# B turned to tokens by a block transposition and SBUF copies instead of four matrix transpositions

## The reference, cut to what matters

```
Y_diag = einsum('bcln,bcsn,bhcls,bcshp->bclhp', C, B, L, x*dt)
states = einsum('bcln,bhcl,bclhp->bchpn',       B, decay, x*dt)
Y_off  = einsum('bcln,bchpn,bhcl->bclhp',       C, states_prev, exp(Acs))
```

## Time and profile before

| | |
|---|---|
| median of 3 runs | 3097.44 us (3097.33 to 3103.48) |
| the profiled execution | 3100.98 us, its span 3099.3 us |
| mean granted TensorE clock | 0.988 of 2.4 GHz |
| TensorE busy | 3020.9 us (97%), 21504 matmuls |
| VectorE busy | 2378.1 us (77%) |
| GpSimd busy | 2047.3 us (66%) |
| ScalarE busy | 1912.2 us (62%) |
| DMA engines, SP's queue | 136608 packets, 210.05 MB, 20.8% of 16 engines |

### The profile page before, as it was taken

How to read it: one execution, slowest core, us unless ns; L and a number is a source line. 1 busy time by engine, 2 the same in 40 slices (tenths; PEclk the granted TensorE clock), 3 DMA queues, 4 the chain that set the end, 5 groups by cost and what they waited for, 6 DMA issues and landing times.

```text
span 3099.3 us, 65999 instructions
## 1 busy us (share of the span) xinstructions
PE 3020.9 (97%) x21504; PEld 2600.8 (84%) x21504; DVE 2378.1 (77%) x5136; ACT 1912.2 (62%) x4117; POOL 2047.3 (66%) x2311
## 2 busy tenths in 40 slices
PE   5799999999999999999999999999999999999997
PEld 4688888888888888888888888888888888888876
DVE  5877887777887778787778777778777778777762
ACT  5566665666666666666566666556666566656562
POOL 2477666677666677666677666677666776666774
PEclk7999999999999999999999999999999999999998
DMA  3123222223222223222222222222222222222221
GB/s 126 42 70 90 75 82 62 68 68 89 75 75 68 68 68 89 75 66 69 70 74 82 79 68 62 65 88 78 79 68 61 68 89 77 80 62 68 68 83 42
DMA packets 153547, 227.36 MB, mean 73 GB/s; under 512 B 30624, under 2 KB 98976, under 8 KB 153504
## 3 DMA queue, kind: packets, MB, share of 16 engines
q1 hardware_dynamic: 136608, 210.05, 20.8%
q0 software_dynamic: 16896, 16.78, 3.8%
HBM read 174.87 MB, written 35.13 MB: 68 GB/s over the span
## 4 chain that ended last, share of the span: by engine, by line
PE 86%; POOL 7%; DVE 1%; issue 1%; DMA 1%; ACT 0%; SPq 0%; POOLq 0%; DVEq 0%; ACTq 0%
PE fpb L1443 32%; PE apb L1443 19%; PE acc L1623 16%; PE apb L1576 4%; PE apb L1452 4%; PE apb L1559 2%; PE ppb L1443 2%; PE apb L1566 2%; POOL hid L653 1%; PE ppb L1462 1%; POOL hidL L658 1%; PE fpb L1492 1%; PE fpb L1494 1%; PE apb L1546 1%; POOL xD L628 1%
## 5 line engine op out<-in xcount | busy, mean ns | idle before, releaser
L658 POOL TENSOR_TENSOR hidL<-hid,hidH 128x512 fp32r<-128x512 f32 x384 | 559.2, 1456 | 204.1 <-ACT hidH L913 196.2
L913 ACT CAST hidH<-hid 128x512 fp32r<-128x512 f32 x384 | 236.6, 616 | 422.0 <-POOL hid L653 312.7
L1129 DVE SCALAR_TENSOR_TENSOR xc<-apb,cw,xc 128x511 f32<-128x511 f32 (+2 forms) x576 | 428.0, 747 | 73.3 <-ACT xc L833 45.4
L1623 PE MATMUL acc<-WDH,hidH 128*128 128x256 f32 x1536 | 457.5, 298 | 5.9 <-POOLq L660 4.8
L1623 PE MATMUL acc<-WDL,hidH 128*128 128x256 f32 x1536 | 430.2, 280 | 0.0
L1623 PE MATMUL acc<-WDH,hidL 128*128 128x256 f32 x1536 | 430.2, 280 | 0.0
L653 POOL TENSOR_TENSOR hid<-hid,cb 128x512 f32<-128x512 f32 x256 | 347.5, 1357 | 40.2 <-DMA cb<-c_row 15.8
L1248 DVE TENSOR_TENSOR hid<-hid,fpb 128x512 f32<-128x512 f32 x384 | 260.2, 678 | 127.4 <-PE fpb L1443 114.6
L1443 PE MATMUL fpb<-fTh,UH 128*128 128x512 f32 x768 | 336.8, 439 | 0.0
L1443 PE MATMUL fpb<-fTh,GH 128*128 128x512 f32 x768 | 317.5, 413 | 0.0
L851 ACT ACTIVATE seg<-seg,acs 128x128 f32<-128x128 f32 x1024 | 313.4, 389 | 4.1 <-POOL seg L613 3.8
(11 more groups left out here) (191 smaller groups left out, 8544.6 us busy)
## 6 DMA issues: line engine op xcount, KB each, us to landing
seg<-acs_row SPq DMA_DIRECT2D x128, 512.0 KB, 4.3
cb<-c_row SPq DMA_DIRECT2D x512, 128.0 KB, 2.9
xsP<-in_x SPq DMA_DIRECT2D x32, 512.0 KB, 3.7
xc<-qrot SPq DMA_DIRECT2D x32, 512.0 KB, 3.4
xc<-in_x SPq DMA_DIRECT2D x32, 512.0 KB, 4.4
out<-xc SPq DMA_DIRECT2D x32, 512.0 KB, 2.9
out<-xn POOLq DMA_DIRECT2D x32, 512.0 KB, 6.1
ZL_loaded<-in_wzx_t SPq DMA_DIRECT2D x2, 512.0 KB, 4.6
```

Of the source, the lines that this page charges most:

```text
L658: own.do(G.tensor_tensor(hidL[:, j % 2, :], hid[:, j % 2, :], hidH[:, j % 2, :].bitcast(fp32), ALU.subtract))
L913: A.copy(hidH[:, j % 2, :], hid[:, j % 2, :]).then_inc(sem["hidden_high"], 1)
L1129: ins = V.scalar_tensor_tensor(xc[:, b, s:], src[:, 0:T - s], cw[:, b, TAPS - 1 - s:TAPS - s], xc[:, b, s:], ALU.mult, ALU.add)
L1623: ins = nc.tensor.matmul(dst, l[:, w, tk], r[:, j, :], start=j == 0 and t % 2 == 0 and n == 0, stop=j == HB - 1 and n == 2, skip_group_che ...
```

## The change

VectorE transposes `xc[:, 4, :]` in 32x32 blocks into `ysp` (`turn_B`), once ScalarE has finished `conv_silu(4)`. Each block is then turned, but lies in the wrong quadrant: 32 channels of quadrant q on the partitions of q. SP issues sixteen DMAs inside SBUF (`spread_B`), one for each pair of quadrants, 32 partitions by 4 chunks by 32 values (16 KB) each, which put the blocks into `Btok`. `state(0)` waits for all sixteen. `B_by_token`, `evac_B` and the slot "Bt" are gone. `turn_B` stands behind `conv(0)` in the loop, behind `conv(1)` in the fill and behind `up(0)` in the tail; `spread_B` stands ahead of `decay_store` everywhere.

```diff
             "qn_ready": ("PE", "p", 2, False), "hh_ready": ("DVE", "p", 2, False),
 
+            "B_made": ("DVE", "a", 1, False), "B_turned": ("SP", "a", 1, False),
+            "B_spread": ("PE", "a", 16 * (P // Q) ** 2, False),
...
+            def spread_B():
+
+                sp.wait_ge(sem["B_turned"], 1)
+                turned = ysp[:].rearrange("p (t u r) -> p t u r", u=P // Q, r=Q)
+                for q in range(P // Q):
+                    for u in range(P // Q):
+                        sp.dma_start(Btok[u * Q:(u + 1) * Q, :, q * Q:(q + 1) * Q], turned[q * Q:(q + 1) * Q, :, u, :]
+                                     ).then_inc(sem["B_spread"], 16)
...
             def first(i):
-                decay_store(); decay_rows(0); load_next(i + 1); decay_rows(1); decay_rows(2); decay_rows(3)
+                spread_B(); decay_store(); decay_rows(0); load_next(i + 1); decay_rows(1); decay_rows(2); decay_rows(3)
...
             def iteration(i, g=True):
-                save_x1(i - 1); decay_store(); decay_rows(0); decay_rows(1); combine_store(); combine_rows(0)
+                save_x1(i - 1); spread_B(); decay_store(); decay_rows(0); decay_rows(1); combine_store(); combine_rows(0)
...
             def conv_silu(b):
                 act.wait_ge(sem["conv_ready"], way.plan.conv.index(b) + 1)
-                free("a", f"xc{b}", A.activation(xc[:, b, :], xc[:, b, :], ACT.Silu))
+                ins = A.activation(xc[:, b, :], xc[:, b, :], ACT.Silu)
+                if b == 4:
+                    own.do(ins)
+                    act.sem_inc(sem["B_made"], 1)
+                    freed["a"].append("xc4")
+                    act.sem_inc(sem["a_out_ACT"], 1)
+                else:
+                    free("a", f"xc{b}", ins)
...
-            def evac_B():
-                way.filled(act, "ACT", "Bt")
-                free("a", "Bt", A.copy(Btok[:].rearrange("p t n -> p (t n)"), way.bank("Bt")[:]))
...
+            def turn_B():
+                dve.wait_ge(sem["B_made"], 1)
+                V.transpose(ysp[:].rearrange("p (b r) -> p b r", r=Q), xc[:, 4, :].rearrange("p (b r) -> p b r", r=Q)
+                            ).then_inc(sem["B_turned"], 1)
...
-            def B_by_token():
-                b = slot("Bt")
-                read_out("xc4")
-                fill("Bt", transposes(b, lambda t: xc[:, 4, t * P:(t + 1) * P]))
...
             def state(c):
                 b = slot(f"st{c}")
                 if c == 0:
-                    read_out("Bt")
+                    pe.wait_ge(sem["B_spread"], 16 * (P // Q) ** 2)
```

More of the change, by code:

```diff
@@ L221, in build @@
                 ("a", "ACT"): (
-                    "za0", "za1", "xc4", "za2", "xc5", "za3", "xc0", "xc1", "zb0", "xc2", "zb1", "Bt", "xc3", "CB",
+                    "za0", "za1", "xc4", "za2", "xc5", "za3", "xc0", "xc1", "zb0", "xc2", "zb1", "xc3", "CB",
                     "zb2", "zb3"),
@@ L239, in build @@
                     ("xc1", "ACT", "ACT"), ("xc2", "ACT", "ACT"), ("CB", "ACT", "ACT"), ("acs", "DVE", "DVE"),
-                    ("Bt", "ACT", "ACT"), ("zb1", "ACT", "ACT"), ("xc3", "ACT", "ACT"), ("zb2", "ACT", "ACT"),
+                    ("zb1", "ACT", "ACT"), ("xc3", "ACT", "ACT"), ("zb2", "ACT", "ACT"),
                     ("zb3", "ACT", "ACT"), ("xt0", "DVE", "DVE"), ("xt1", "DVE", "DVE"), ("st0", "DVE", "DVE"),
@@ L970, in iteration @@
                 if g: final_norm()
-                conv_first(3); round_hidden(1); silu_z(1, 1); round_hidden(2); evac_B(); conv_silu(3); gate(3)
+                conv_first(3); round_hidden(1); silu_z(1, 1); round_hidden(2); conv_silu(3); gate(3)
                 gate(4); evac_CB(); silu_z(2, 1); exp_table(); decays(); exp_seg(0); round_hidden(3)
@@ L989, in tail @@
                 silu_table(); gate(2); conv_silu(1); final_norm(); evac_CB(); conv_silu(2); exp_table()
-                decays(); round_hidden(1); evac_B(); silu_table(); silu_z(1, 1); gate(3); round_hidden(2)
+                decays(); round_hidden(1); silu_table(); silu_z(1, 1); gate(3); round_hidden(2)
                 conv_first(3); silu_z(2, 1); round_hidden(3); gate(4); conv_silu(3); silu_z(3, 1)
@@ L1354, in iteration @@
                 if g: final_moments()
-                dt_finish(); conv(0); up(0); conv(1); conv(2); route_scores(); evac_acs(); up(1)
+                dt_finish(); conv(0); turn_B(); up(0); conv(1); conv(2); route_scores(); evac_acs(); up(1)
                 route_groups(); up(2); conv(3); route_experts(); up(3); times_dt(0); times_dt(1); decay_CB(0)
@@ L1657, in first @@
                 project_z(2, 1); project_x(1); cumulate(); project_x(2); settled("ad_ready"); project_x(3)
-                project_z(3, 1); x_by_token(0); CB(); x_by_token(1); B_by_token(); state(0); diagonal(0)
+                project_z(3, 1); x_by_token(0); CB(); x_by_token(1); state(0); settled("B_spread"); diagonal(0)
                 state(1); from_state(1); diagonal(1); x_by_token(2); from_state(2); state(2); x_by_channel(0)
@@ L1676, in iteration @@
                 gate(1); up(1); project_z(0, 1); cumulate(); gate(2); settled("ad_ready"); project_z(1, 1)
-                project_x(3); up(2); gate(3); down(0); settled("acc_free"); B_by_token(); project_z(2, 1)
+                project_x(3); up(2); gate(3); down(0); settled("acc_free"); project_z(2, 1)
                 gate(4); CB(); x_by_token(0); up(3); down(1); x_by_token(1); down(2)
-                up(4); gate(5); state(0); project_z(3, 1); diagonal(0); up(5)
+                up(4); gate(5); state(0); settled("B_spread"); project_z(3, 1); diagonal(0); up(5)
                 from_state(1); state(1); down(3); x_by_token(2); gate(6); diagonal(1); from_state(2); up(6)
@@ L1696, in tail @@
                 project_x(1); up(1); project_x(2); gate(2); up(2); CB(); gate(3); cumulate(); down(0)
-                settled("ad_ready"); settled("acc_free"); B_by_token(); project_z(1, 1); up(3); project_x(3)
+                settled("ad_ready"); settled("acc_free"); project_z(1, 1); up(3); project_x(3)
                 project_z(2, 1); down(1); gate(4); project_z(3, 1)
-                up(4); x_by_token(0); gate(5); x_by_token(1); down(2); up(5); state(0); diagonal(0); state(1)
+                up(4); x_by_token(0); gate(5); x_by_token(1); down(2); up(5); state(0); settled("B_spread"); diagonal(0); state(1)
                 from_state(1); gate(6); diagonal(1); down(3); y_by_channel(0); x_by_token(2); from_state(2)
```

16 lines of the change are left out of this document (8 added, 8 removed).

## The result

The changed kernel takes 3104.36 us (median of 12 runs, 3100.01 to 3106.57), the kernel before, run beside it, 3097.78 (12 runs, 3092.94 to 3103.48). The ratio is 1.0022, 95% interval 1.0014 to 1.0029: slower by 6.6 us, where 8.7 us less was forecast. The profiled execution took 3104.4 us (span 3102.7), 3.4 us more than that of before, and this difference can be traced.

What follows compares the result with a forecast made beforehand. The prediction took TensorE to bound the 30 iterations, with GpSimd nearly as tight, and the fill to be a chain of waits. -13.2 (TensorE) + 4.2 (fill) + 0.3 (tail) = -8.7 us, giving 3088.7 us; range 3083 to 3103.

Steps and rivals of the forecast that it cites:

- hidden, but with little to spare: Loop, GpSimd: mask(1) ends between 1088.5 and 1090.2, before decayed(0) at 1090.38; cover 0.2 to 1.9 us, no cost.
- 8.9 us for sixteen: SP's queue ahead of decay_store: sixteen copy issues at 0.555 us each, 8.9 us in all.
- the two now start together: Loop: decay loads, from 1079.8 instead of 1077.20, start with the result store of 1079.28; together 7.25 us of DMA work.
- the ends given: SP's price per copy issue: 0.40 to 0.73 us, making the fill's loss 1.7 to 7.0 us.
- the store's head start: Loop, worst case: all of it (2.24 less 0.5) competes, so the second decay load lands 1.7 us later, at 1089.1.
- So the second load lands at 1087.4: Loop: second decay load lands 7.6 us after the first is issued, as in the tail; at worst at 1089.1.
- rival A: Fill: it absorbs its delay, leaving -13.2 + 0.3, so 3084.5 us; chance 0.08.
- The fill, 4.2 forecast: Fill: decay_store 9.35 us later, 3.9 absorbed, diagonal(0) at 74.45 instead of 70.24, so 4.2 us lost.
- TensorE's 0.44: Loop, TensorE: four transpositions removed save 0.44 us in each of 30 iterations, 13.2 us.
- gated(0)'s pause of 0.16: Loop, GpSimd: the pause of 0.60 us before gated(0) shrinks to 0.16, so the 0.44 just fits.
- Rival B: Loop, GpSimd held in mask(1) or result_stored; delay d changes an iteration by d - 0.60; 3113.9 us at d = 1.0; chance 0.14.
- rival C: Loop: d, decayed(0)'s delay, near 0.5; 30 x -0.10 + 4.5 = +1.5, so no change, 3098.9 us; chance 0.14.

Runs made afterwards that it cites:

- fourteen copies ahead: Changed kernel, in the loop alone fourteen copies issued ahead of the decay store and two behind the decay loads: 3096.25 us in one execution (before 3102.73).
- the loop's split: Changed kernel, in the loop alone nine copies issued ahead of the decay store and seven behind the two decay loads: ratio 0.9982, median 3094.47 us.

## Why the prediction was wrong

**What failed is the step that called the wait for the decay loads "hidden, but with little to spare". Its first term, sixteen SP issues at 0.555 us, "8.9 us for sixteen", was too small.** They take 0.65 each, 10.4 in all. In the loop that is the difference between "the two now start together", as the prediction had the loads and the store, and loads 2.1 us behind the store. The run with fourteen copies ahead is, in the loop, the kernel that was forecast: SP free at +3.1 (forecast +2.9), loads at +5.1 (+4.9), and there the whole gain arrives. The price 0.65 was within the ends given (0.40 and 0.73), but these ends went only into the fill's part of the range; in the loop the worst case was taken from the store's head start alone.

**The step from there to decayed(0) was too short as well.** "So the second load lands at 1087.4", and mask(1) ends between 1088.5 and 1090.2: this added mask(1)'s 1.09 to the landing, as if mask(0) were done by then. mask(0) waits for the first load, which lands behind the store too, and then mask(0), hold_shift and mask(1) take 2.47 us in a row. In the times of before the run of mask(0) starts between 1087.7 and 1089.2, so decayed(0) lies between 1090.2 and 1091.7, where 1090.2 was the worst. The price of the issues alone would not have shown this: with 0.65 in the prediction's own sum the loads leave at +6.45, the second lands 7.6 us later at +14.05, and mask(1) ends at +15.1, still ahead of VectorE's +15.44. And the landing varies by 1.5 us from iteration to iteration, which a single sum can't show; what makes it vary was not found.

**How the engines share.** The prediction let the store and the loads compete on equal terms. The Trainium skill, "DMA: Bandwidth & Descriptors" (Queues, rings and completion order), says that each engine takes turns between the queues it has work for, packet by packet. With fourteen copies ahead the trace agrees for a part: 0.44 and 0.57 MB beside each other from 1090 to 1095, but only once the store has been kept out for some 2 us by the loads, whose packets start first. In the changed kernel, where the store's start first, it does not: 523 packets of the store pass beside 25 of SP's in 4 us, though the loads are issued at 1090.24 and by the 0.97 above their packets could start at 1091.2. Why the later queue gets no turn at first was not found. The Trainium skill, on the same page (Issuing engines are not separate DMA queues), says that the sequencer's time is usually small beside the DMA; the prediction drew rival A's 3084.5 from it. Here it is not small: 10.4 us of issue for sixteen transfers of 16 KB.

**The fill, 4.2 forecast, 9.0 measured at the first mark.** By its own steps: turn_B ended 0.95 us later than worked out (conv(1) was 0.93 later in this execution); the issues took 1.5 more; the decay load took 4.54 us from issue to mask(0) where it had taken 3.60, 0.94 more; together 3.4, so diagonal(0) was 7.8 late instead of 4.2. Behind it came what was not in the sum: 1.2 more until the first mark. The 1.6 of TensorE's clock behind that mark belong to the execution, not to the change: they come with early fills too and are missing with late ones.

**What was right.** TensorE's 0.44 per iteration (0.46), and that all of it can arrive; gated(0)'s pause of 0.16 behind it (0.13 to 0.16 in nearly all iterations with the loop's split); turn_B in VectorE's pause (0.67 forecast, 0.70); ScalarE, PSUM's ring and state(0) without cost in the loop. Rival B named the place, GpSimd held behind the decay loads beside the accumulating store, at a chance of 0.14; its formula, an iteration changed by d - 0.60, gives 93.69 + 0.73 = 94.42 for the iteration shown with decayed(0) at +16.77 (d = 1.33, from +15.44 before); it took 94.09. Over the 29 iterations d is 0.54 in the mean, which is rival C's case in the loop (-0.10 us an iteration; measured -0.23). That the whole is slower than C's 3098.9 comes from the fill.

**What the profile had shown and was not read.** "30 iterations go at TensorE's pace" was half of it. Of the 29 iterations before, 20 took 0.39 us longer than the short ones, because a down projection that waits for GpSimd's rest starts 0.3 to 0.4 us later, at 74 us behind acsT; the trace shows hardly any idle time of TensorE there (0.06 us in such an iteration), so its busy time of 93.57 hid it. The row of GpSimd's 0.60 us before gated(0) said that it had next to no slack; it had none at the other end.

That the medians differ by 6.6 us and the profiled executions by 3.4 stays partly open: GpSimd's slow instruction alone can move an execution by 29 x 0.40 = 11.6 us, a fall of the clock as above by 1.6, and their share in the runs without a profile is not known.

## What to carry to other kernels

Count the issues that a change puts ahead of a wait at what such an issue takes in a row of its own kind, and carry both ends of that price through every stage, not only the one with the obvious delay. A load that is issued a little later lands much later when it falls behind another transfer: write down which transfers start in that stretch and in which order. Where many small issues are not urgent, put those that don't fit into the queue's idle time behind the urgent load: nine ahead and seven behind, with turn_B moved ahead in the fill, turned +0.2% into -0.5%. A lower clock in one execution is not yet the price of a change: look for it in the executions of the other versions first.

## What the runs showed of the hardware

- Sixteen copies inside SBUF of 128 runs of 128 bytes took SP 0.65 us each (10.41), one transfer of the whole 256 KB 0.5.
- A store issued 2.1 us ahead of two loads of another queue kept them out of the engines until nearly all of it was done; issued 0.8 us ahead of them, it was itself kept out for some 2 us. The loads' first packets come 0.97 us after their issue, this store's 1.95.
- A GpSimd instruction of 0.19 us took 0.33 to 0.52 when a VectorE instruction with two operands in SBUF had started 0.19 to 0.01 us ahead: it ended 0.05 us after that one. The Trainium skill, "GPSIMD Engine Reference" (Specifications), says that GpSimd's way to SBUF is shared with VectorE for such instructions; the rows agree, and add the price.
